# Conditioned residual on one core: groups of five batches instead of four in each transfer

## What is computed

```python
W = weights[condition]                       # one 128 x 128 matrix for each batch
out = x + jnp.einsum('bct,bcd->bdt', x, W)   # x plus the matrix applied along the channels
```

## Time and profile before

| | us |
|---|---|
| median of 3 runs | 319.81 (319.79 to 320.04) |
| profiled execution | 320.25 |
| its span, first to last instruction | 318.5 |
| matmuls (PE) busy | 250.5 |
| DVE busy | 146.8 |
| POOL busy | 18.9 |

### The profile page before, as it was taken

How to read it: one execution, slowest core, us unless ns; L and a number is a source line. 1 busy time by engine, 2 the same in 40 slices (tenths; PEclk the granted TensorE clock), 3 DMA queues, 4 the chain that set the end, 5 groups by cost and what they waited for, 6 DMA issues and landing times.

```text
span 318.5 us, 1353 instructions
## 1 busy us (share of the span) xinstructions
PE 250.5 (79%) x512; PEld 106.3 (33%) x512; DVE 146.8 (46%) x65; POOL 18.9 (6%) x69
## 2 busy tenths in 40 slices
PE   0099999990896959959698695987949689696990
PEld 0044444440342424424243242433414234242430
DVE  0026766762074552525527174262735607347252
POOL 0000010010000010100100000000000100000000
PEclk9999999998598997969989798797989969789798
DMA  8999999999999999999999999999999999999997
GB/s 329 424 432 453 346 453 451 403 453 403 453 416 449 444 412 453 403 457 432 428 449 407 449 420 440 449 412 453 407 453 416 444 449 407 453 403 457 436 393 302
DMA packets 5323, 135.29 MB, mean 425 GB/s; under 512 B 586, under 2 KB 714, under 8 KB 842
## 3 DMA queue, kind: packets, MB, share of 16 engines
q1 hardware_dynamic: 2448, 68.16, 50.0%
q10 hardware_dynamic: 2874, 67.11, 49.0%
HBM read 68.16 MB, written 67.11 MB: 425 GB/s over the span
## 4 chain that ended last, share of the span: by engine, by line
DMA 62%; PE 33%; DVE 3%; issue 0%; SPq 0%
PE product L92 33%; DMA x_ring<-x 31%; DMA out<-x_ring 30%; DVE x_ring L108 3%; SPq L58 0%
## 5 line engine op out<-in xcount | busy, mean ns | idle before, releaser
L92 PE MATMUL product<-x_ring,chosen_weights 128*128 128x512 f32 x512 | 250.5, 653 | 59.9 <-DMA x_ring<-x 59.9
L108 DVE TENSOR_TENSOR x_ring<-product,x_ring 128x2048 f32<-128x2048 f32 x64 | 146.7, 2292 | 163.8 <-PE product L92 163.8
L92 PEld LDWEIGHTS product<-x_ring,chosen_weights 128*128 128x128 f32 x512 | 106.3, 210 | 203.2 <-issue 125.0
L80 POOL COPY chosen_weights<-weight_table 128x128 f32 x64 | 18.7, 293 | 287.1 <-DVE x_ring L108 280.2
L102 DVE TENSOR_SCALAR state_row<-condition_row 1x64 int32<-1x64 int32 x1 | 0.2, 182 | 2.0 <-DMA condition_row<-condition 2.0
L144 POOL MEMSET const-float32-0.0<- 128x1 f32 x1 | 0.1, 98 | 0.1
L144 POOL MEMSET const-bfloat16-1.0<- 128x1 bf16 x1 | 0.1, 102 | 0.0
L144 POOL MEMSET const-uint8-127<- 128x1 uint8 x1 | 0.1, 102 | 0.0
L144 POOL MEMSET const-float32-1.0<- 128x1 f32 x1 | 0.1, 98 | 0.0
L144 POOL BASE_LOAD x1 | 0.0, 12 | 0.1
## 6 DMA issues: line engine op xcount, KB each, us to landing
x_ring<-x SPq DMA_DIRECT2D x16, 4096.0 KB, 28.5
out<-x_ring ACTq DMA_DIRECT2D x15, 4096.0 KB, 30.2
out<-x_ring ACTq DMA_DIRECT2D x3, 1024.0 KB
weight_table<-weights SPq DMA_DIRECT2D x1, 1024.0 KB, 4.8
out<-x_ring ACTq DMA_DIRECT2D x1, 896.0 KB
out<-x_ring ACTq DMA_DIRECT2D x1, 124.0 KB
condition_row<-condition ACTq DMA_DIRECT2D x1, 0.2 KB
out<-x_ring ACTq DMA_DIRECT2D x1, 4.0 KB
```

The source lines that it names most:

```text
L80: pool.tensor_copy(chosen_weights[b][:, :], weight_table[:, bass.ds(state[b] * features, features)]).then_inc(weights_chosen[b], 1)
L92: last = pe.matmul(product[:, b % psum_slots, m * BANK_COLUMNS:(m + 1) * BANK_COLUMNS], chosen_weights[b][:, :], x_ring[:, bass.ds(b * tim ...
L108: dve.tensor_tensor(tile, product[:, b % psum_slots, :], tile, AluOpType.add).then_inc(sum_done[b], 1)
```

## The change

A group is five batches (40 KB rows), 12 such groups and a last one of four batches (32 KB rows). Since the last group is shorter, `x` and `out` are flat in memory and `rows` makes the view of each group. The rooms stay four, so the ring grows from 128 to 160 KB a partition. `chosen_weights` goes from 16 tiles to 4. PE, POOL and DVE loop over 20 batches, three turns, and then do the remaining four batches behind the loop. The last group is again stored batch by batch, in the same six DMAs.

```diff
-GROUP = 4
+GROUP = 5
 ROOMS = 4
...
+    group_columns = GROUP * time
+    groups = -(-batches // GROUP)
+    short = batches - (groups - 1) * GROUP
...
-    turns = batches // per_turn
+    turns, rest = divmod(batches, per_turn)
+    weight_slots = 4
+
+    def rows(flat, g):
+        count = GROUP if g < groups - 1 else short
+        start = g * GROUP * channels * time
+        return flat[start:start + count * channels * time].rearrange("(c t) -> c t", c=channels)
...
-        chosen_weights = [sbuf(f"chosen_weights{b}", [channels, features]) for b in range(per_turn)]
+        chosen_weights = [sbuf(f"chosen_weights{b}", [channels, features]) for b in range(weight_slots)]
...
             for g in range(groups):
                 room = g % ROOMS
+                source = rows(x, g)
                 if g >= ROOMS:
                     sp.wait_ge(room_stored[room], 16 * (g // ROOMS))
-                sp.dma_start(x_ring[:, room * group_columns:(room + 1) * group_columns], x[g]
-                             ).then_inc(x_loaded[g % ROOMS], 16)
+                column = room * group_columns
+                sp.dma_start(x_ring[:, column:column + source.shape[1]], source).then_inc(x_loaded[room], 16)
...
+            with pool.Fori(0, turns) as turn:
+                choose(turn, per_turn)
+            choose(turns, rest)
...
+            with pe.Fori(0, turns) as turn:
+                multiply(turn, per_turn)
+            multiply(turns, rest)
...
             with dve.Fori(0, turns) as turn:
-                for b in range(per_turn):
...
+                add(turn, per_turn)
+            add(turns, rest)
...
-                act.dma_start(out[g], x_ring[:, room * group_columns:(room + 1) * group_columns]
+                act.dma_start(rows(out, g), x_ring[:, room * group_columns:(room + 1) * group_columns]
                               ).then_inc(room_stored[room], 16)
...
-            for i in range(GROUP):
+            target = rows(out, g)
+            for i in range(short):
```

More of the change, by code:

```diff
@@ L8, with conditioned_residual @@
 PSUM_BANKS = 8
-GROUP = 4
+GROUP = 5
 ROOMS = 4
-def conditioned_residual(nc, x, condition, weights, out):
+def conditioned_residual(nc, x, condition, weights, out, batches, time):
     fp32 = mybir.dt.float32
[L15 to L18, removed]
+    channels, states, features = weights.shape
+    group_columns = GROUP * time
+    groups = -(-batches // GROUP)
+    short = batches - (groups - 1) * GROUP
     matmuls = time // BANK_COLUMNS
@@ L154 @@
     out = nc.dram_tensor("out", arrays["x"].shape, mybir.dt.float32, kind="ExternalOutput").ap()
-    conditioned_residual(nc, *args, out)
+    conditioned_residual(nc, *args, out, batches, time)
     result = run_bass_kernel_spmd(nc, [arrays], core_ids=[0])
-    grouped = result.results[0]["out"].reshape(batches // GROUP, channels, GROUP, time)
-    return np.ascontiguousarray(grouped.transpose(0, 2, 1, 3)).reshape(batches, channels, time)
+    flat = result.results[0]["out"]
+    parts, start = [], 0
+    for b in range(0, batches, GROUP):
+        count = min(GROUP, batches - b)
+        part = flat[start:start + count * channels * time].reshape(channels, count, time)
+        parts.append(part.transpose(1, 0, 2))
+        start += part.size
+    return np.concatenate(parts)
```

33 lines of the change are left out of this document (21 added, 12 removed).

## The result

The changed kernel is slower and, above all, scattered: median 322.58 us (320.11 to 326.14, 15 executions) against 319.89 us (319.57 to 321.32, 15 executions) before. The ratio is 1.006, 95% interval 1.004 to 1.008; it leaves out the two longest executions of the changed kernel (325.21 and 326.14 us) and is therefore milder than the medians. Two later sets of the same kernel gave 322.60 and 322.40 us. The forecast was 319.25 us, with 318.5 to 320.5 as its range.

The account below looks back on a forecast made before the run. The prediction took bytes through full DMA engines as the bound. From the median 319.81 us it subtracted 0.55 us for fewer packets, with start, middle and tail at zero, giving 319.25 us, range 318.5 to 320.5.

Parts of the forecast that it names:

- What bounds the kernel: Whole span: DMA engines are full, so bytes bound it; 135.29 MB at 433 GB/s are 312.4 of 318.5 us.
- Fewer, longer packets: Loads and stores: 48 fewer packets an engine at 11.5 ns each, saving 0.55 us, all on the path.
- Start and middle: First group and steady course: later first store, at 39.1 us, but engines never lack work; no cost, no gain.
- Tail: End of kernel: earlier last sum closes the gap at 313 us; worth 0 to 0.12 us, taken as 0.
- Sum: Whole kernel: 0.55 us saved from the median 319.81 us gives 319.26, so 319.25 us.
- A: Rival at the tail: late engines finish together without the gap, 0.65 us more gain, 318.6 us; chance 0.18.
- B: Rival on packets: a packet costs next to nothing, 319.6 to 319.8 us; chance 0.19.
- C: Slower rival at loop ends: instruction blocks fetched again through the DMA engines, up to + 1.8 us, 321.05 us; chance 0.12.
- D: Slower rival on rows: each 40 KB row cut in two packets, 1.66 us more, 321.5 us; chance 0.06.

Follow-up runs that it names:

- e13: Changed kernel written out without loops on PE and VectorE, first group of four batches, then twelve of five: 320.05 us, ratio 1.0006 against the kernel before.
- e17: Written out without loops, one group of four then twelve of five, with the fifth load also waiting for the 13th sum: 320.19 us.
- e11: Changed kernel written out without loops, groups of 2, 3, 4, then eleven of five: 320.20 us, ratio 1.0006 against the kernel before.
- e15: Changed kernel with the first group stored in two pieces, four batches and then the fifth: 320.29 us, ratio 1.001 against the kernel before.
- e3: Changed kernel, groups of five, with rows starting 48 KB apart in memory: 320.51 us, ratio 1.0026 against the kernel before.
- e5: Changed kernel with each group loaded by two DMAs, of three and two batches, stores whole: 330.62 us.
- e6: Changed kernel with each whole group stored by two DMAs, of three and two batches, loads whole: 326.53 us.
- e12: Changed kernel's sizes, twelve groups of five and one of four, written out without loops: 323.41 us, ratio 1.0092 against the kernel before.

## Why the prediction was wrong

- *What bounds the kernel.* Right as far as it went: the middle has share 1.00 and the bytes set the time. It stopped at the mean of 16 engines.
- *Fewer, longer packets.* Right in the count, 2016 packets, and near in the saving. A packet costs about 8 ns beside its bytes where I took 11.5, so 48 packets are 0.38 us, and six fewer completion records of 9 ns an engine are 0.05 more. Net of stretched packets each engine has 0.52 us less to do, forecast 0.55; what the last 0.1 us is isn't shown. The Trainium skill's page "DMA: Bandwidth & Descriptors", section "Why small descriptors are slow", has about 3 cycles a packet; at the 850 MHz that the page gives for the fabric that is, as an estimate, 3.5 ns. The measured 8 ns are more than twice that.
- *Start and middle.* No bubble at full cover, as worked out (the first store was issued at 40.5 us, forecast 39.1). But "Cost nothing" was a statement on engines without work. It did not ask whether packets of the new length keep their duration. Between 55 and 95 us they don't, by 0.9 us in the quick profiled execution.
- *Tail.* Right in mechanism: the gap at 313 us is gone, and it brings nothing. The sizes were off: the last load landed at 289.7 us (281.5 to 285 forecast), the last sum ended at 307.8 us (299 to 305), and the share was 0.95 and not 1.00 in 314 to 316 us. One term was mis-sized, the time that the store queue has the engines to itself after the first four loads: 2.6 us in my sum and 8.8 us in the trace; the trace of before had 8.6 us to read. Between issue and first packet lie 4 us (68.38 and 72.44 us), where I took 1.5 for a store. "An engine that finishes late had no gap" held the clue, and I used it for the tail alone.
- *Sum.* The failed step: "as the engines are the bound all of it is on the path". 48 packets are saved on each engine, but the end is that of the last engine, and packets did not keep their durations. In the profiled executions of the table the last load's lag, 1.7 and 2.7 us with groups of four, was 2.3 to 7.1 us in the kernels with groups of five, and the mean work, 314.7 and 315.2 us with fours, was up to 317.4 us.
- *Rivals.* A didn't happen, and B's free packet didn't either (8 ns). C didn't: one block of code, and four in the written out kernels without a visible price. D, the row cut in two, didn't. The case that came, engines drifting apart, was not among them, and so the chance of slower was 0.15. A rival with it could have been had from the trace of before: the piece from 35 to 39 us at 393 GB/s with a share over 1 showed that packets stretch when a transfer starts beside the other queue. I priced it at 0.4 us, as a constant.

What stays open: why packets stretch between 50 and 95 us, and single engines fall behind, when the first group is five batches stored whole, and why this is rare with 32 KB rows and wasn't seen with 24 KB ones (eight executions). An empty load queue is not the cause by itself; the row distance in memory may shift how often it happens; an earlier first store goes with less of it. None of the kernels with fives beats the one before: the best, 320.05 us (e13), 320.19 (e17), 320.20 (e11) and 320.29 (e15), are level with it. The lowest single executions of groups of five, 319.42 (e3) and 319.50 us (e15), are 0.07 to 0.15 us under the lowest of before (319.57).

## To carry to other kernels

With the DMA engines full, the time is that of the slowest of the 16, not of their mean: read the last microseconds of the DMA share, and time a kernel often enough to see its scatter, before a saving on each engine is counted in full. Beyond 32 KB a longer row had almost nothing left to save here (8 ns in 1213) and brought variance. If longer rows are wanted, a smaller first group kept the time steady here (e11, e13), though no better than groups of four. Rows of the two queues should have the same length: engines take them packet for packet, and the two runs with unequal rows (e5, e6) had over 7 us of stretched packets an engine.

## What the runs showed of the hardware

- A row is one packet up to 48 KB at least; durations 309, 1213, 1514 and 1815 ns for 8, 32, 40 and 48 KB.
- Packets of two queues alternate one for one (64 beside 66 between 45 and 55 us in e5): 24 and 16 KB against 40 KB rows gave 40 to 53 us to landing on the one queue and 23 to 25 us on the other, and cost 2 to 3% (ratios 1.0334 and 1.0205).
- A lag mostly stays once it is there: in the kernel before it is 1.9 us from 81 to 158 us and 2.7 at the end; in e12 it grows from 3.0 at 100 us to 7.1. It can shrink too: in e17 from 2.4 us at 66 us to 0.9 at 93 us.
- From the issue of a load or store on an empty queue to its first packet it took 4 us while the other queue kept the engines busy (40.51 to 44.56 us, a store, and 68.38 to 72.44 us, a load, in the changed kernel), and 1.0 us with idle engines (0.80 to 1.81 us, the weights).
- Single packets can take twice their time (3076 in place of 1514 ns) on a few engines, around the moment at which a transfer starts beside the other queue (e12, fifth load).
